# Norm statistics taken where x is made, and x loaded inside the first stage

## The reference

```
def _layernorm(x, axis=-1, eps=1e-05):
    m = jnp.mean(x, axis=axis, keepdims=True)
    v = jnp.var(x, axis=axis, keepdims=True)
    return (x - m) / jnp.sqrt(v + eps)

x = x + 0.5 * _L0_ffn_ref(_layernorm(x), ...)    # low-rank stage: W, and A/Bmat/LiMEs with a soft choice
x = x + _L0_attn_ref(_layernorm(x), ...)         # 32 heads of 16, causal, with a 10-token adapter prefix
x = x + 0.5 * _L0_ffn_ref(_layernorm(x), ...)
x = x + 0.5 * _L1_ffn_ref(_layernorm(x), ...)    # 16 experts, top 2, and a shared part
x = x + _L1_attn_ref(_layernorm(x), ...)         # 32 query heads, 8 key/value heads of 128
x = x + 0.5 * _L1_ffn_ref(_layernorm(x), ...)
```

## Time and profile before

| | |
|---|---|
| median of 3 runs | 1802.05 us (1801.62 to 1803.87) |
| profiled execution | 1799.84 us |
| its span | 1798.1 us |
| busy in the span: PE, DVE, ACT, POOL | 89%, 56%, 50%, 55% |
| mean granted clock of TensorE | 0.946 |

### The profile page before, as it was taken

How to read it: one execution, slowest core, us unless ns; L and a number is a source line. 1 busy time by engine, 2 the same in 40 slices (tenths; PEclk the granted TensorE clock), 3 DMA queues, 4 the chain that set the end, 5 groups by cost and what they waited for, 6 DMA issues and landing times. The chain is left out here.

```text
span 1798.1 us, 26487 instructions
## 1 busy us (share of the span) xinstructions
PE 1606.9 (89%) x8164; PEld 1242.7 (69%) x8164; DVE 1004.5 (56%) x2630; ACT 900.9 (50%) x1876; POOL 984.8 (55%) x1122
## 2 busy tenths in 40 slices
PE   5597899998768998589999999999999999979996
PEld 4486555546547886467878788787878778757884
DVE  5561556551657236655656565656565656665235
ACT  3112565652221231477777776777677777731230
POOL 2252555541221443378787877777878777812533
PEclk9798789988879999899999999999999999989999
DMA  2200000000134933244544353444434344463834
GB/s 85 91 10 3 2 3 2 3 3 1 37 141 154 339 133 111 85 107 108 115 111 114 82 136 89 107 108 103 122 91 127 81 100 89 91 229 121 318 119 139
DMA packets 312096, 180.24 MB, mean 100 GB/s; under 512 B 281895, under 2 KB 283767, under 8 KB 309568
## 3 DMA queue, kind: packets, MB, share of 16 engines
q1 hardware_dynamic: 300160, 152.81, 30.5%
q0 software_dynamic: 11840, 26.25, 4.7%
HBM read 111.08 MB, written 22.54 MB: 74 GB/s over the span
## 5 line engine op out<-in xcount | busy, mean ns | idle before, releaser
L1325 POOL TENSOR_TENSOR st_prob<-st_prob,st_rinv 128x512 f32<-128x512 f32 x256 | 266.3, 1040 | 177.0 <-DVE st_rinv L1393 177.0
L1329 POOL TENSOR_TENSOR st_plane<-st_prob,st_plane 128x512 f16<-128x512 f32 x256 | 307.6, 1211 | 0.3 <-ACT st_plane L1245 0.3
L1245 ACT ACTIVATE st_plane<-st_prob 128x512 f16<-128x512 f32 x256 | 161.2, 630 | 126.9 <-POOL st_prob L1325 126.8
L1261 ACT ACTIVATE st_prob<-st_score,st_nmax 128x512 f32<-128x512 f32 x256 | 175.2, 685 | 59.8 <-DVE st_nmax L1400 57.2
L1400 DVE TENSOR_REDUCE st_nmax<-st_score 128x1 f32<-128x512 f32 x256 | 175.1, 684 | 41.5 <-PE st_score L108 38.6
L2038 DVE CUSTOM_DVE_ANT_0 st1b_dump<-st1b_score,st1b_maskrow 128x128 f32<-128x128 f32 (+3 forms) x256 | 112.7, 487 | 95.5 <-PE st1b_score L1736 68.9
L1240 ACT ACTIVATE st_pthi<-st_plane_t 128x512 fp32r<-128x512 f16 x256 | 159.5, 623 | 3.4 <-DMA st_plane_t<-st_plane 3.2
L1370 DVE CAST st_ptlo<-st_plane_t 128x512 fp32r<-128x512 f16 x256 | 148.9, 582 | 2.6 <-DMA st_plane_t<-st_plane 2.6
L1374 DVE TENSOR_TENSOR st_olo<-st_outp,st_ohi 128x512 fp32r<-128x512 f32 x64 | 44.2, 690 | 166.8 <-ACT st_ohi L1249 166.8
L1893 ACT ACTIVATE st1b_slabs<-st1b_across 128x512 f32<-128x512 f32 (+1 forms) x192 | 90.6, 526 | 90.4 <-PE st1b_across L1755 70.1
L106 PE MATMUL st_outp<-st_pthi,st_vhi 128*128 128x512 f32 x256 | 103.8, 406 | 28.4 <-ACT st_pthi L1240 27.4
(11 more groups left out here) (380 smaller groups left out, 4056.3 us busy)
## 6 DMA issues: line engine op xcount, KB each, us to landing
st_raw<-in_moe_w SPq DMA_DIRECT2D x40, 768.0 KB, 7.3
sorted_outs<-st_ln_xn SPq DMA_DIRECT2D x62, 256.0 KB, 4.1
st_qraw<-in_gqa_q SPq DMA_DIRECT2D x8, 1024.0 KB, 5.4
st_oraw<-in_gqa_o SPq DMA_DIRECT2D x8, 1024.0 KB, 5.3
rows<-st_ln_xn SPq DMA_DIRECT2D x2, 2048.0 KB, 9.3
st_kvraw<-in_gqa_kv SPq DMA_DIRECT2D x8, 512.0 KB, 3.9
st_plane_t<-st_plane SPq DMA_TRANSPOSE x256, 2.7
st1a_raw<-in_w_attn SPq DMA_DIRECT2D x3, 1024.0 KB, 6.6
```

The lines of the kernel that those rows point to most:

```text
L1245: act.activation(plane[t][:, 0:T], prob[:, t, :], ACT.Copy).then_inc(upper_ready, 1)
L1261: act.activation(prob[:, t, :], score[t][:, :], ACT.Exp, bias=nmax[:, slot:slot + 1], accum_out=rsum[:, slot:slot + 1]).then_inc(exp_ready, 1)
L1325: pool.tensor_tensor(prob[:, t, :], prob[:, t, :], rinv[:, slot:slot + 1].broadcast_to([P, T]), ALU.mult).then_inc(norm_ready, 1)
L1329: pool.tensor_tensor(plane[t][:, T:2 * T], prob[:, t, :], plane[t][:, 0:T], ALU.subtract).then_inc(lower_ready, 1)
```

## The change

The statistics (`bn_stats`, `bn_aggr`) leave `Norm.vector_rows` and go to a new class `Moments`. Each stage that makes x takes them on DVE for the stage behind it, one tile after the other as the additions finish, and aggregates them at its end. `stats` and `mv` are now tiles that live for the whole program. ACT calculates one square root of a column of `ident` into an unused tile at the end of its list (in st1c, whose ACT list was empty, at its start; in st0 also once at its head). `load_stage` is gone: st0 issues eight transfers of x (256 KB each), then ident, and then its own weights, and takes the statistics of each tile as it lands. st5 keeps its old end.

```diff
-def load_stage(nc, env, dram):
-    with ExitStack() as ctx:
-        s = Stage(nc, ctx, "load")
-        loaded = s.sem("loaded")
-        with nc.Block() as block:
-
-            @block.sync
-            def _(sp):
-                sp.dma_start(env["ident"][:, :], dram["ident"]).then_inc(loaded, 16)
-                sp.dma_start(env["x"][:, :, :], dram["x"].rearrange("(t p) c -> p t c", p=P)).then_inc(loaded, 16)
-                sp.wait_ge(loaded, 32)
+class Moments:
+
+
+    def __init__(self, s, env):
+        self.x, self.stats, self.mv = env["x"], env["stats"], env["mv"]
+        self.stats_ready, self.mv_ready = s.sem("stats_ready"), s.sem("mv_ready")
+        self.table, self.ident = env["table"], env["ident"]
+
+    def take(self, dve, t):
+        dve.bn_stats(self.stats[:, t, :], self.x[:, t, :]).then_inc(self.stats_ready, 1)
+
+    def close(self, dve):
+        dve.wait_ge(self.stats_ready, NT)
+        for t in range(NT):
+            dve.bn_aggr(self.mv[:, t, :], self.stats[:, t, :]).then_inc(self.mv_ready, 1)
+        dve.wait_ge(self.mv_ready, NT)
+
+    def root_table(self, act):
+        act.activation(self.table[:, :], self.ident[:, 0:1], ACT.Sqrt)
 
 
 class Norm:
 
     def __init__(self, s, env, banks, rows=None):
         self.x, self.xhi, self.xlo, self.ident, self.bank = env["x"], env["xhi"], env["xlo"], env["ident"], banks
-        self.stats, self.mv = s.sb("ln_stats", [P, NT, 6]), s.sb("ln_mv", [P, NT, 2])
+        self.mv = env["mv"]
         self.ve, self.sd = s.sb("ln_ve", [P, NT]), s.sb("ln_sd", [P, NT])
         self.ra, self.rb, self.rc = s.sb("ln_ra", [P, NT]), s.sb("ln_rb", [P, NT]), s.sb("ln_rc", [P, NT])
...
     def vector_rows(self, dve):
         x, mv, ve, ra, rb, rc = self.x, self.mv, self.ve, self.ra, self.rb, self.rc
-        for t in range(NT):
-            dve.bn_stats(self.stats[:, t, :], x[:, t, :]).then_inc(self.stats_ready, 1)
-        for t in range(NT):
-            dve.wait_ge(self.stats_ready, t + 1)
-            dve.bn_aggr(mv[:, t, :], self.stats[:, t, :]).then_inc(self.mv_ready, 1)
-        dve.wait_ge(self.mv_ready, NT)
         dve.tensor_scalar(ve[:, :], mv[:, :, 1], 1e-5, None, ALU.add).then_inc(self.var_ready, 1)
         dve.wait_ge(self.std_ready, 1)
         dve.reciprocal(ra[:, :], self.sd[:, :]).then_inc(self.rstd_step, 1)
...
+        first = name == "st0"
+        norm, moments = Norm(s, env, bank), Moments(s, env)
+        if first:
+            entry, ident_loaded, x_loaded = Moments(Stage(nc, ctx, "entry"), env), s.sem("ident_loaded"), [s.sem(f"x_loaded{n}") for n in range(NT)]
...
             @block.sync
             def _(sp):
+                if first:
+                    for t in range(NT):
+                        sp.dma_start(x[:, t, :], dram["x"][t * P:(t + 1) * P, :]).then_inc(x_loaded[t], 16)
+                    sp.dma_start(ident[:, :], dram["ident"]).then_inc(ident_loaded, 16)
                 sp.dma_start(a_t[:, :], dram["a_t"]).then_inc(a_loaded, 16)
...
                 pe.wait_ge(aw_ready, 3)
+                if first:
+                    pe.wait_ge(ident_loaded, 16)
                 norm.tensor(pe)
...
+                if first:
+                    act.wait_ge(ident_loaded, 16)
+                    entry.root_table(act)
                 act.wait_ge(al_ready, 1)
...
                 act.wait_ge(wtt_ready, 1)
                 act.activation(wt_t[0:E0, :], bank[1][0:E0, :], ACT.Copy).then_inc(wtt_copied, 1)
+                moments.root_table(act)
...
+                if first:
+                    for t in range(NT):
+                        dve.wait_ge(x_loaded[t], 16)
+                        entry.take(dve, t)
+                    entry.close(dve)
                 norm.vector_rows(dve)
...
@@ -409,6 +429,12 @@
                     dve.wait_ge(bias_added, j + 1)
                     dve.scalar_tensor_tensor(out=x[:, order[j], :], in0=wide[j % 6][:, :], scalar=0.5, in1=x[:, order[j], :],
                                              op0=ALU.mult, op1=ALU.add).then_inc(x_added, 1)
+                    if j >= 1:
+                        dve.wait_ge(x_added, j)
+                        moments.take(dve, order[j - 1])
+                dve.wait_ge(x_added, NT)
+                moments.take(dve, order[NT - 1])
+                moments.close(dve)
...
+        norm, moments, last_stage = Norm(s, env, bank), Moments(s, env), name == "st5"
...
                         act_hi(i)
+                if not last_stage:
+                    moments.root_table(act)
...
                             add_step(i - 1)
                             if i > ends_at and i < NI - 1:
                                 combine(4)
-                add_step(NI - 1)
-                combine(2 * NT)
+                if last_stage:
+                    add_step(NI - 1)
+                    combine(2 * NT)
+                else:
+                    combine(2 * NT)
+                    for t in range(TB):
+                        add_step(NI - 1, 1)
+                        wait(dve, *written[t])
+                        moments.take(dve, t)
+                    for t in range(TB, NT):
+                        wait(dve, *written[t])
+                        moments.take(dve, t)
+                    moments.close(dve)
...
                 for t in range(TB):
                     turned_hi(LAST, NU - 1, t)
                 out_hi(LAST, NU - 1)
+                moments.root_table(act)
...
                 add(KV1, 0)
                 for t in range(TB):
                     turned_lo(LAST, NU - 1, t)
+                wait(dve, o_added, outs(KV1, 1))
+                for t in range(TB):
+                    moments.take(dve, t)
                 out_lo(LAST, NU - 1)
                 for u in range(1, 5):
                     add(KV1, u, score[u - 1])
+                    if u >= 2:
+                        wait(dve, o_added, outs(KV1, u))
+                        moments.take(dve, TB + u - 2)
+                wait(dve, o_added, outs(KV1, 5))
+                moments.take(dve, NT - 1)
+                moments.close(dve)
...
 
+            @block.scalar
+            def _(act):
+                moments.root_table(act)
+
             @block.vector
             def _(dve):
                 for t in range(NT):
                     dve.wait_ge(out_ready, t + 1)
                     dve.tensor_tensor(x[:, t, :], bank[t % 4][:, :], x[:, t, :], ALU.add).then_inc(added, 1)
+                    if t >= 1:
+                        dve.wait_ge(added, t)
+                        moments.take(dve, t - 1)
+                dve.wait_ge(added, NT)
+                moments.take(dve, NT - 1)
+                moments.close(dve)
...
+        env["stats"], env["mv"] = s.sb("stats", [P, NT, 6]), s.sb("mv", [P, NT, 2])
+        env["table"] = s.sb("table", [P, 1])
         env["xd"] = nc.dram_tensor("rows", (NT * P, C), F32, kind="Internal").ap()
         env["ys"] = nc.dram_tensor("sorted_outs", (TILES * P, C), F32, kind="Internal").ap()
         Stage.used = []
-        load_stage(nc, env, dram)
         for n, stage in enumerate((lime_ffn_stage, adapter_attention_stage, lime_ffn_stage, moe_stage, gqa_stage, moe_stage)):
             stage(nc, env, dram, f"st{n}")
```

More of the change, by code:

```diff
@@ L139, in __init__ @@
         self.rows = rows
-        self.stats_ready, self.mv_ready, self.var_ready, self.std_ready = (s.sem(n) for n in ("ln_stats_ready", "ln_mv_ready", "ln_var_ready", "ln_std_ready"))
+        self.var_ready, self.std_ready = s.sem("ln_var_ready"), s.sem("ln_std_ready")
         self.rstd_step, self.xn_ready, self.turned_ready = (s.sem(n) for n in ("ln_rstd_step", "ln_xn_ready", "ln_turned_ready"))
@@ L213, in lime_ffn_stage @@
         bank = [s.ps(f"bank{n}", [P, 512]) for n in range(8)]
-        norm = Norm(s, env, bank)
+        first = name == "st0"
+        norm, moments = Norm(s, env, bank), Moments(s, env)
+        if first:
+            entry, ident_loaded, x_loaded = Moments(Stage(nc, ctx, "entry"), env), s.sem("ident_loaded"), [s.sem(f"x_loaded{n}") for n in range(NT)]
         w_loaded, a_loaded, c_loaded = s.sem("w_loaded"), s.sem("a_loaded"), s.sem("c_loaded")
@@ L1000, in gqa_stage @@
         outp = [s.ps(f"outp{n}", [P, T]) for n in range(2)]
+        moments = Moments(s, env)
         norm = Norm(s, env, [qbank, sbank] + score + outp, [prob[:, t, :] for t in range(TB)] + [raw["o"][:, t * C:(t + 1) * C] for t in range(TB)])
```

## The result

The changed kernel takes **1816.09 us** (median of 5 runs, 1804.90 to 1823.86) against 1802.05 for the kernel before (median of 5, 1798.82 to 1806.54, on the same chip). The ratio is 1.0072, 95% interval 1.0045 to 1.0099: slower by 0.7%. Forecast were 1795.1 us and a range of 1790.5 to 1799.7.

What follows compares the result with a forecast made beforehand. PE was taken to set the time inside stages and to stand still at their heads while `Norm` works. Terms -3.9 - 2.1 - 1.0 + 2.5 - 2.8 + 0.3 = -7.0 on 1802.05 gave 1795.1 us, range 1790.5 to 1799.7.

Steps and rivals of the forecast that it cites:

- entry: Start and st0's head: x issued first in eight pieces, w lands earlier; -3.9 us, bounds -3.2 and -4.5.
- st1a: Head of st1a: scaling finishes before the weights land, which then come last; -2.1 us, bounds 1.7 and 2.3.
- st2: Head of st2: scaling begins as before, POOL's L336 later; -1.0 us, the middle of -2.5 and +0.45.
- st3: Head of st3: root waits behind the gate weights' split, whose transfer starts later; +2.5 us, bounds +2.2, +2.9.
- st4: Head of st4: scaling and transposes finish earlier, then q's split and the low parts; -2.8 us, gain 2.1 to 3.1.
- st5: Head of st5: split, then root and scaling, start later as in st3; +0.3 us, 0.1 to 0.6.
- st2's coin: Whether st2's eighth tile starts scaling before POOL's L336: -2.5 us if it passes, +0.45 if caught; even chance each.
- Rival 3: TensorE's clock in st1b: four further pairs at the lower level, +12, make the kernel slower, +5, 1807 us; 6%.
- Rival 2: Entry gives little (-0.5; slow pieces or w queued) and st2's tile is caught: 1799.9 us, no measurable change; 14%.
- Rivals 1 and 4: 1: borders gain what was moved, 1789.3 us, 8%. 4: Sqrt table loaded again before the root, 1800 us, 4%.

Runs made afterwards that it cites:

- e2: Kernel before with one unused tile of 32 B a partition behind xlo: 1821.28 us, ratio 1.0081.
- e3: Kernel before with one unused tile of 64 B a partition behind xlo: 1816.40 us, ratio 1.0060.
- e4: Kernel before with only the entry's edit (x in eight transfers inside st0) and a `table` of 64 B: 1812.97 us, ratio 1.0048.
- e1: Changed kernel with `table` made 16 columns wide (64 B a partition instead of 4): 1810.86 us, ratio 1.0048.
- e6: Kernel before with one unused tile of 128 B a partition behind xlo: 1819.99 us, ratio 1.0087.
- e8: Kernel before with only the entry's edit and a `table` of 128 B: 1814.29 us, ratio 1.0064.
- e7: Changed kernel with `table` made 32 columns wide (128 B a partition): 1815.23 us, ratio 1.0058.
- e5: Kernel before itself, nothing changed, on another chip: 1804.57 us, ratio 0.9999.
- e9: Kernel before with one unused tile of 256 B a partition behind xlo: 1806.22 us, ratio 1.0021.
- e11: Kernel before with only the entry's edit and a `table` of 512 B: 1804.25 us, ratio 1.0022.
- e10: Changed kernel with `table` made 64 columns wide, stages' tiles 512 B later than in the kernel before: 1804.21 us, ratio 1.0008.
- e13: The kernel of e10 once more, nothing changed: 1802.03 us, ratio 0.9990.
- e12: Kernel before with 32 B unused ahead of x, so that no tile moves against another: 1802.70 us, ratio 1.0006.
- e17: e15 with the statistics for st2 taken in st1c again and the Sqrt table loaded there: 1795.78 us, ratio 0.9969.
- e15: e10 with statistics and Sqrt table back in the norm for st2, st3 and st5: 1796.38 us, ratio 0.9956.
- e16: e15 with unused tiles, 192 B ahead of weights' buffers in st3 and st5, 128 B ahead of st4's probability tiles: 1790.10 us, ratio 0.9933.
- e18: e15 with the statistics for st3 taken in st2 again and the Sqrt table loaded there: 1799.57 us, ratio 0.9998.

## Why the prediction was wrong

**The step that failed** is one that the prediction doesn't write down: it takes the duration of every body from the rows of before, as if only heads could change. The sum has no term for the 288 B that `stats`, `mv` and `table` put ahead of the stage tiles. Its size: 1.0072 with them, 1.0008 and 0.9990 at 512 B, some 13 us. That the places cost it is shown by kernels in which nothing else differs, and by the change and the unchanged kernel at the same places (within 256 B):

| the stages' tiles moved by | unchanged kernel | entry alone | whole change |
|---|---|---|---|
| 32 B (288) | 1.0081 (e2) | | 1.0072 |
| 64 B (320) | 1.0060 (e3) | 1.0048 (e4) | 1.0048 (e1) |
| 128 B (384) | 1.0087 (e6) | 1.0064 (e8) | 1.0058 (e7) |
| 0 (256, 512) | 0.9999, 1.0021 (e5, e9) | 1.0022 (e11) | 1.0008, 0.9990 (e10, e13) |

Of the causes behind the places, the spacing of products is shown (e2, e3, e6 without the change, e9 and e12 as controls); the slower transfers are shown, and shown to cost little (e12). The spacing may not be all of it. The mean granted clock was 0.940 in the median of the changed kernel's runs and 0.939 in that of e2, e3 and e6, against 0.942 to 0.944 before. At 0.941 the kernel before ran 15 times, in 1803 to 1808 us, and the changed one once, in 1816.1; at 0.944 16 times, in 1798 to 1804 us, and the changed one once, in 1804.9. So at one clock the change costs 3 to 10 us, and a part of the loss, by these rows perhaps half (an estimate), comes with the lower clock. Whether the places bring that about too is open.

**The terms, in the changed kernel's own trace:**

| term | forecast | measured | from |
|---|---|---|---|
| entry | -3.9 | -3.7 | start to st0's first product, 28.34 and 24.63 |
| st1a | -2.1 | -1.8 | first of six additions to first product, 22.97 and 21.21 |
| st2 | -1.0 (-2.5 or +0.45) | -2.05 | last addition to first product: 454.87 to 473.73 is 18.86, 451.15 to 467.96 is 16.81; the tile passed |
| st3 | +2.5 (bound +2.9) | +2.9 | first of six additions to the scaling, 12.29 and 15.19 |
| st4 | -2.8 | -2.3 | first of four additions to first product: 717.9 to 739.54 is 21.6, 715.33 to 734.65 is 19.3 |
| st5 | +0.3 | +0.05 | 1584.46 to 1602.79 and 1587.81 to 1606.19 |

Their sum is -6.9, forecast -7.0. No table load stands in a head, and in st1a, st2, st3 and st5 what came last is what the forecast named. That the sums agree so closely is luck in part. st2's tile passed here and was caught in each of the other five traces that could show it (below). Of the entry's 3.7 us, 3.15 stand at the scaling; from there to the first product unchanged kernels differ by 0.8 us among themselves (10.8 to 11.6), which is more than the other 0.55.

**But heads aren't the time.** With the places restored, the changed kernel is at 1.0008 and 0.9990 where the sum says 0.996. In the table above the change gains 0.09, 0.12, 0.29 and (of the means) 0.11% over the unchanged kernel at the same places, on average 0.15%, an estimate of 3 us with an uncertainty about as large; the forecast's 7 us lie outside it. The entry alone has -0.12, -0.23 and (against the mean of e5 and e9) +0.12%: that leaves anything from nothing to the forecast's 3.9 us. What is seen in the traces:

- st2's coin. In e1, e7, e10, e13 and e17 POOL was first and the scaling took 8.2 to 8.3 us; the changed kernel's trace passed by a tenth of a microsecond. In those five the last addition to the first product took 19.4 to 20.0 us, against 18.7 to 19.6 in the unchanged kernels. The even chance was too kind: the kernel lost the toss five times in six.
- The clock around an earlier start. The 4 us before st1a's first product and the 4 us after it, in e9, in e13 and in e10, which is the same kernel as e13 (PE, PEld, DVE, ACT, POOL busy (count), PEclk, DMA share, GB/s):

```profile
86.88:90.88 4.00, 4.00 (x24) 4.00 (x23) 3.21 (x5) 2.97 (x6) 0.00 (x0) 0.59 1.06 423
90.88:94.88 4.00, 4.00 (x21) 3.30 (x20) 2.73 (x4) 3.12 (x4) 1.15 (x1) 1.00 0.09 37
```

```profile
81.38:85.38 4.00, 0.39 (x5) 0.15 (x3) 4.00 (x7) 4.00 (x8) 3.95 (x1) 1.00 0.05 14
85.38:89.38 4.00, 4.00 (x12) 3.15 (x13) 3.30 (x3) 1.38 (x2) 2.90 (x1) 0.63 0.63 190
```

```profile
81.72:85.72 4.00, 0.94 (x9) 0.69 (x7) 4.00 (x7) 4.00 (x8) 3.95 (x1) 1.00 0.05 14
85.72:89.72 4.00, 4.00 (x17) 3.30 (x18) 3.31 (x3) 1.38 (x2) 2.90 (x1) 1.00 0.64 199
```

  In e9 the clock was at 1.2 GHz for most of the 4 us before, under the transposes, and back at 2.4 when the products came. In e13 the transposes were done early, PE stood nearly idle with the clock at 1.00, and then the half clock met the products: the body of st1a takes 1.6 us more (e13, e15 and e17; in the changed kernel's trace it stands beside the wider spacing). In e10, e16 and e18 it doesn't, but there the stretch before, from st0's first product to st1a's, takes 0.8 to 1.8 us more than in those three. From st0's first product to st1b's it is 138.4 us in before, e9 and e12 (137.6 in e5) and 137.3 to 138.1 in the six: of the head's 1.8 us, 0.3 to 1.1 are left.
- The same at the start of st1c: 44.7 to 44.9 us to st2's first product in e13 and e15, 41 in before and e9. e12, an unchanged program, had 44.5: an accident of the clock as well. The end, from st5's first product, took 196.6 to 197.2 in e10, e11, e13, e17 and e18 and 195.0 to 195.5 in before, e5, e9 and e12, but 195.6 and 194.2 in e15 and e16. Why is open.

That these three make up the whole missing gain is worked out from single traces, not shown. Times of one program on one chip spread over 15 to 20 us with the mean clock (the kernel before: 1792.8 us at 0.951, 1813.4 at 0.937), and st1b alone took 257.0 us in e10 and 271.3 in e15 at the same instructions; the prediction's "runs differ by about 1 us either way" rested on three runs. Its range is also 0.4 us lower than its own bounds with that 1 us give (1791.0 to 1800.0), which changes nothing.

**The rivals.** Rival 3, slower by the clock in st1b, named the right side and not the main cause: st1b was shorter in the changed kernel's trace (263.1 us against 266.1). That trace is of its fastest run, though, and the clock was lower in the other four. Rival 2 said the entry gives little; in e11 nothing of it shows in the time, but in the changed kernel's trace x's last piece was used at 9.79 us (forecast 9.1) and w at 12.90 (forecast 12.3, before 16.02), so pieces that flow slowly are not the reason. Rivals 1 and 4 didn't occur.

## What to carry to other kernels

A change that adds or resizes a permanent tile moves all tiles behind it: work out by how many bytes, and compare the spacing of products before blaming the edit. A control is cheap: the unchanged kernel with an unused tile of the same size. Where TensorE is the bound, try to let both operands of a product begin at the same place within 256 B; unused tiles do it, and here gave 0.4% without touching an instruction. Statistics are worth moving only where nothing else in the next head comes last: into st3 here (from st3's first product to st4's 203 to 205 us, before 205 to 209), not into st2, where the border cost 2.7 us. What moving them into st0 won was for the greater part lost again around the clock.

## What the hardware showed unasked

- Products of 128x512 (fp32r) stood 226.5 ns apart with xhi, xlo and the weights at one place within 256 B, 234 with the stages' tiles 32 or 288 B later, 229 with 64 or 320, 232 with 128 or 384, 227 with 256 or 512. The Trainium skill ("TensorE: Matmul & The Clock Gate", "Step-by-step: what each phase is for") says that PE reads its two operands through two independent ports and that loading weights takes nothing from the running product; by that one would not look for an effect of one operand's place against the other's, and here it is up to 7 ns a product. By what way it comes about no run shows. The rule isn't complete either: scores in st4, with both operands in stage tiles, went from 227 to between 230 and 234 ns when both moved together by 128 B (e6). What else takes part was not tried.
- The queue with the transposed transfers took 43 to 44% of its engines' time in 900 to 1500 us with the stages' tiles shifted by 0, 256 or 512 B and 49 to 50% with 32, 64, 128, 288, 320, 384, or with everything 32 B later. The Trainium skill ("DMA: Bandwidth & Descriptors", "How a descriptor splits into AXI transactions") says that a descriptor off a 256 B boundary is charged for the bytes before it, back to the boundary. The period seen here agrees; the amount doesn't follow, since 32, 64 and 128 B cost alike (49.3, 49.2 and 49.5%).
- The half clock (1.2 GHz) fell on the transposes ahead of st1a's first product (0.59 in the 4 us before it, e9) or on its first products (0.63 in the 4 us after, e13), but in the same kernel another time not on the products (1.00, e10). An earlier start of a stage can meet the slower level and give back part of what it won.
